# Attention with relative positions and a ternary layer: one PSUM bank moved from the small products to the logits, all places set anew

## The chip, the cores and the metric

The kernel runs on one core of a Trainium2 chip. The metric is the time of one launch on the device, in microseconds (us), as the median of several runs. The engines are TensorE (PE in the profile, with PEld for its weight loads, which overlap the products), VectorE (DVE), ScalarE (ACT), GpSimd (POOL) and SyncE (SP, whose queue issues the DMAs). Each works its own instructions strictly in order and waits on semaphores for the others. PSUM, the memory into which PE writes, has eight banks here, each of 128 partitions x 512 float32.

## The reference

Eight sequences of 1024 tokens with 256 features, 16 heads of 16, go through attention with learned relative positions (clipped at 64) and then through a linear layer with ternary weights; each has a layer norm ahead and behind.

```python
B, S, H, NH, MRP = 8, 1024, 256, 16, 64            # DK = 16
idx = clip(r[None, :] - r[:, None], -MRP, MRP) + MRP
rk, rv = embK[idx], embV[idx]                       # (S, S, DK)
q, k, v = heads(x @ Wq.T + bq), heads(x @ Wk.T + bk), heads(x @ Wv.T + bv)
logits = einsum('bhqd,bhkd->bhqk', q, k) + einsum('bhqd,qkd->bhqk', q, rk)
w = softmax(logits, axis=-1)
out = einsum('bhqk,bhkd->bhqd', w, v) + einsum('bhqk,qkd->bhqd', w, rv)
attn = out @ Wo.T + bo
x = x + layernorm(attn(layernorm(x)))
w_ternary = where(weight > delta, 1, where(weight < -delta, -1, 0))   # delta = 0.7 * mean(|weight|)
x = x + layernorm(layernorm(x) @ (w_ternary * alpha).T + bias)
```

## The kernel before

**Steps.** The attention runs over 128 steps: 8 sequences (batches) x 2 groups of 8 heads x 8 tiles of 128 queries. Four steps make a quad. A step s has these stages, and each is code in several engines' programs:

- row_max (s, p, half): PE multiplies keys and queries into the two banks of scores (L919); VectorE reduces each bank to a maximum per query, with the band of relative positions added (L1222, the near half) or without (L1216, the far half). There are eight such pairs of banks in a step.
- max_rows: PE turns the maxima (L929, into a misc bank), VectorE splits them into nm (L1235, L1237), and SyncE moves them into qs.
- weights (s, head, X or Y): PE makes a block of transposed logits for four or eight keys' tiles, four heads side by side, in a bank of logitsT (L946); the two nearest tiles get their band added through an identity product (L950). ScalarE takes the exponential into wl, wm, wr or wy (L1424) and so frees the bank. A half step has four X blocks, of which the first two are banded, and four Y blocks.
- weighted: PE multiplies the weights with the values into oacc (L970). merge: VectorE joins wl and wm (L1245).
- band_raw: PE makes the raw band terms for later steps in a misc bank (L902), ScalarE copies them twice into praw (L1403, L1404), and SyncE writes them to memory (bs, L785) and reads them back skewed (bands, L798).

Per quad come relative (L982, VectorE L1254), relative_sum (L995, VectorE adds it into oT, L1263) and out_norm (L1006, VectorE L1279). Beside the loop run the projections of the next batch in four chunks (turn_x L865, project_q and project_k L875, far L883, project_v L892 with VectorE's L1195) and the tail of each tile with both linear layers (tail_attT and tail_x1T L1020, tail_wo and tail_ff L1034 with VectorE's L1292 and L1333).

**PSUM.** The eight banks are NSCORE = 2 for scores, NLOG = 2 for logitsT, one for oacc and NMISC = 3 for misc. Scores and logits take their banks in turn. PE waits, before block n of logits, for exponential n - NLOG:

```python
lt = logitsT[block % NLOG]
pe.wait_ge(exp_ready, block + 1 - NLOG)
```

All small products (band_raw, max_rows, relative, relative_sum, out_norm, the projections, far and the four products of a tail; 993 uses of a bank in all) share the misc banks.

**The order.** Nothing is scheduled on the chip. The table PLACES gives every stage a place on a line, in slots of which a step has eight; timetable() lays all stages of all steps, chunks and tails out by it, and order_of() sorts them for each engine, with an offset for some stages on some engines (LAG, and END_LAG for the last four tiles). Each engine's program is its own sorted list. with_banks() goes through the same list and gives each small product the misc bank that comes free first. For that it assumes that a use holds its bank for HOLD[stage] slots; where no bank is free at its place, the stage and the rest of its chain are put off on the line:

```python
bank = until.index(min(until))
if until[bank] > slot:
    if chain:
        late[chain] = until[bank] - planned
    put_back((until[bank], i, planned, stage, k))
    continue
...
until[bank] = slot + (10 if stage == "relative" and k[2] < 3 else HOLD[stage])
```

HOLD and PLACES only set the order and the banks. On the chip PE always waits for the instruction that really frees the bank (misc_banks() makes that list from the plan, `pe.wait_ge(*free)`).

Of the kernel before, what the change touches and what calls it, by code (L numbers as in the profile page):

```python
# [11 lines left out]
ACT = mybir.ActivationFunctionType  # L12
# [33 lines left out]
LOWEST = -3.0e38  # L46
QRING, BRING, VRING, MRING = 5, 7, 3, 3
HB = HG // 2
NLOG, NMISC, NSCORE = 2, 3, 2


def tile_of(s):
# [51 lines left out]
def own_root(stage, k):  # L104
# [1 line left out]
    return k == (0, 0) if stage == "statistics" else last_tile(*k) and k[1] % 2 == 1  # L106


PLACES = {'chunk': (61.05, 71.03, 81.0, 91.0),
 'load_x': -8.23,  # L110
 'statistics': -5.34,
 'normalise': -2.6,
 'turn_x': 0.38,
 'project_q': 1.18,
 'project_v': 10.3,
 'far': 4.0,
 'write_q': 6.3,
 'project_k': 5.53,
 'write_far': 7.8,
# [4 lines left out]
 'first_stages': (-0.27, 0.5, 2.6, 4.4, 4.8, 5.83, 6.2, 6.3),  # L124
 'keys_first_stages': (0.0, 4.0, 4.8, 0.0, 3.0, 8.5, 7.3, 5.33),
 'first_load_k': (-84.0, -73.9, -63.8, -62.01),
 'first_load_q': (-89.0, -77.2, -65.4, -53.6),
 'first_raw': -54.47,
 'step': 7.2,
 'half': 3.55,  # L130
 'load_k': (-41.8, -33.8, -25.8, -17.8),
 'first_load_mk': (-83.9, -73.8, -63.8, -63.5),
 'load_mk': (-41.7, -33.7, -25.7, -17.7),
 'load_mq': -21.5,
 'first_load_mq': (-88.17, -77.1, -65.3, -53.5),
 'load_q': -32.7,
 'raw': (-28.8, -25.4),
 'band_write': (-26.3, -22.8),
 'band_read': (-22.18, -20.26),
 'row_max': (-12.49, -11.62, -10.75, -9.88, -9.01, -8.14, -7.1, -6.4),  # L140
 'max_reduce': -6.0,
 'max_rows': -4.88,
 'max_move': -5.05,
 'near': (0.0, 0.4, 0.72, 0.98),
 'rest': (1.76, 2.1, 2.5, 2.9),
 'value_x': 2.3,
 'value_y': 4.1,
 'merge': 3.2,
 'out_copy': 7.6,
 'relative': (29.57, 31.07),  # L150
 'piece_by': 0.35,
 'sum': (33.0, 33.95),
 'norm': (35.6, 36.59),
 'tail': 38.0,
 'tail_by': 8.0,
 'tail_late_by': 6.5,
 'tail_load': -1.0,
 'tail_attT': 0.21,
 'tail_wo': 1.0,
 'tail_x1': 3.0,  # L160
 'tail_norm': 3.5,
 'tail_normed': 5.4,
 'tail_x1T': 10.15,
 'tail_ff': 11.3,
 'tail_out': 13.5,
 'tail_store': 15.82,
 'end': 36.6,
 'end_by': 0.65,
 'end_stages': (0.3, 0.41, 2.27, 2.4, 3.4, 4.3, 4.7, 7.0, 6.8)}


def timetable():

    slots, x_ = [], PLACES

# [92 lines left out]
def with_banks(slots):  # L268
# [12 lines left out]
    while queue:  # L281
        slot, i, planned, stage, k = queue.pop()
        chain, bank = chain_of(stage, k), None
        if slot < planned + late.get(chain, 0):
            put_back((planned + late[chain], i, planned, stage, k))
            continue
        if stage in HOLD:
            if stage == "relative" and k[2]:
# [17 lines left out]
 'DVE': {'project_v': 0.17,  # L306
         'out_norm': 0.7,
         'tail_wo': 0.7,
         'tail_x1': 1.06,
         'tail_norm': 1.4,  # L310
         'tail_normed': 3.2,
         'tail_out': 1.9},
 'ACT': {'turn_x': -0.23, 'far': 0.4, 'project_q': 1.2, 'band_raw': -0.04},
 'POOL': {'project_q': 3.4,
          'project_k': 2.0,
          'far': 2.0,
# [6 lines left out]

END_LAG = {'PE': {},
 'SP': {},
 'DVE': {'tail_wo': 0.28, 'tail_ff': 0.5},
 'ACT': {'tail_attT': 0.2, 'tail_x1T': 1.0},
 'POOL': {'tail_wo': 0.95, 'tail_norm': 0.35, 'tail_ff': 0.86}}

# [1 line left out]
def order_of(engine, slots):  # L331


    def lag(stage, k):
# [25 lines left out]
HOLD = {'turn_x': 0.8,  # L360
 'project_q': 2.0,
 'project_k': 2.0,
 'far': 1.4,
 'project_v': 1.8,
 'band_raw': 0.8,
 'max_rows': 0.9,
 'relative': 1.0,
 'relative_sum': 1.4,
 'out_norm': 1.83,
 'tail_attT': 0.6,  # L370
 'tail_x1T': 0.5,
 'tail_wo': 1.3,
 'tail_ff': 1.3,
 'ternary': 2.0}


def counts(orders):
# [1186 lines left out]
```

## Time and profile before

| | |
|---|---|
| median of 3 runs | 2714.83 us (2706.01 to 2718.36) |
| the profiled execution | 2715.1 us |
| its span | 2713.3 us |
| TensorE busy | 2488.4 us, 92% |
| VectorE busy | 2098.3 us, 77% |
| ScalarE busy | 1563.9 us, 58% |
| GpSimd busy | 949.4 us, 35% |
| DMA engines busy with the main queue | 57.3% |

Busy times are of the whole span. The first 100 us are the start (constants, the first batch's projections, the first scores), the last 70 us the end of the last tiles; between them PE runs nearly full. A row of the timeline gives start and duration, the engine, the source line, the operation, output <- inputs by name and the count of merged instructions; in brackets stands the idle time before it and who ended that. Products are pipelined: neighbouring rows of PE overlap by up to some 0.1 us.

### The profile page before, as it was taken

To read this page: it belongs to the slowest core of one execution; us is meant where nothing else is said; L and a number is where in the kernel's file an instruction comes from. 1 tells how busy PE (TensorE), PEld (TensorE's weight loads), DVE (VectorE), ACT (ScalarE), POOL (GpSimd) and SP (SyncE) were. 2 spreads that over 40 slices of the span, in tenths; PEclk is the share of its full clock that TensorE was granted. 3 is DMA by queue.
4 is the path that set the end of the run, shared out by engine and by line. 5 is a ranking of instruction groups with operands and counts; after the bars stand their busy time and mean duration, and the time that the engine had idled before them with its cause. 6 is when DMAs were issued, how large, how long until landed. Compare 5 with 4: busy or idle time off the path is not lost. (4 is left out here: it accounts for less than half of the span.)

```text
span 2713.3 us, 101117 instructions
## 1 busy us (share of the span) xinstructions
PE 2488.4 (92%) x41858; PEld 1778.2 (66%) x41858; DVE 2098.3 (77%) x5306; ACT 1563.9 (58%) x2993; POOL 949.4 (35%) x2211
## 2 busy tenths in 40 slices
PE   5599999999999999999999999999999999999995
PEld 3266766667666676667666676666766667666664
DVE  5577778877888778877788777887778877787776
ACT  2266665566666555666556665556665655566652
POOL 3001533335342443424334253343524244341014
PEclk8699999999999999999999999999999999999997
DMA  6765674657656575566655666456764657656510
GB/s 162 210 162 160 184 185 132 163 161 204 167 148 168 156 196 155 148 164 178 183 140 157 172 187 177 138 145 167 209 168 132 164 168 192 164 141 178 142 42 29
DMA packets 696147, 434.22 MB, mean 160 GB/s; under 512 B 215847, under 2 KB 695431, under 8 KB 695559
## 3 DMA queue, kind: packets, MB, share of 16 engines
q1 hardware_dynamic: 695686, 427.75, 57.3%
q8 instruction: 330, 5.41, 0.9%
q14 instruction: 131, 1.07, 0.1%
HBM read 231.91 MB, written 194.92 MB: 157 GB/s over the span
## 5 line engine op out<-in xcount | busy, mean ns | idle before, releaser
L946 PE MATMUL logitsT<-qs,ks 98*128 98x128 bf16 (+1 forms) x8192 | 952.9, 222 | 31.5 <-ACT wr L1424 11.6
L1222 DVE CUSTOM_DVE_ANT_1 junk<-scores,bands 128x512 bf16<-128x512 f32 x988 | 680.3, 689 | 270.4 <-PE scores L919 115.4
L1424 ACT ACTIVATE wy<-logitsT 128x512 f32<-128x512 f32 x1024 | 589.5, 597 | 419.8 <-PE logitsT L946 408.7
L1216 DVE TENSOR_REDUCE maxes<-scores 128x1 f32<-128x512 f32 x1024 | 657.3, 683 | 173.3 <-PE scores L919 171.0
L946 PEld LDWEIGHTS logitsT<-qs,ks 98*128 98x128 bf16 (+1 forms) x8192 | 576.0, 99 | 306.6 <-issue 172.2
L919 PE MATMUL scores<-mks,mqs 48*128 48x256 bf16 (+6 forms) x3712 | 518.8, 291 | 121.1 <-DVE maxes L1216 62.5
L950 PE MATMUL logitsT<-ident,bands 128*128 128x128 f32 x2048 | 407.9, 280 | 0.0
L1424 ACT ACTIVATE wr<-logitsT 128x512 f32<-128x512 f32 x512 | 293.5, 596 | 163.6 <-PE logitsT L946 157.4
L919 PEld LDWEIGHTS scores<-mks,mqs 48*128 48x128 bf16 (+1 forms) x3712 | 162.9, 94 | 333.7 <-DVE maxes L1216 111.2
L1453 POOL TENSOR_SCALAR rs<-rs 128x1 int32<-128x1 int32 (+1 forms) x217 | 42.2, 195 | 898.9 <-DVE rs L1097 888.4
L950 PEld LDWEIGHTS logitsT<-ident,bands 128*128 128x128 f32 x2048 | 295.8, 144 | 24.9
L1458 POOL TENSOR_SCALAR rs<-rs 128x1 f32<-128x1 f32 x744 | 282.4, 382 | 64.9
L970 PE MATMUL oacc<-wy,vs 128*17 128x128 f32 (+1 forms) x9216 | 277.1, 264 | 0.7 <-ACT wy L1424 0.7
L1463 POOL TENSOR_SCALAR rs<-rs 128x1 f32<-128x1 f32 x744 | 217.5, 295 | 66.1
L970 PEld LDWEIGHTS oacc<-wy,vs 128*17 128x17 f32 x9216 | 207.1, 98 | 37.5 <-issue 9.4
L1424 ACT ACTIVATE wl<-logitsT 128x512 f32<-128x512 f32 x256 | 158.4, 619 | 117.7 <-PE logitsT L950 116.4
L1424 ACT ACTIVATE wm<-logitsT 128x512 f32<-128x512 f32 x256 | 154.3, 603 | 83.0 <-PE logitsT L950 78.4
L1403 ACT ACTIVATE praw<-misc 128x512 f32<-128x512 f32 x256 | 153.4, 599 | 64.7 <-DMA bs<-praw 44.0
L1245 DVE COPY_PREDICATED wm<-later,wl 128x512 f32<-128x512 int32 x224 | 175.7, 784 | 2.2 <-PE oacc L970 2.2
L970 PE MATMUL oacc<-wr,vs 128*17 128x128 f32 (+1 forms) x4608 | 161.6, 264 | 0.0
L1404 ACT ACTIVATE praw<-misc 128x512 f32<-128x512 f32 x256 | 156.3, 611 | 0.0
L970 PEld LDWEIGHTS oacc<-wr,vs 128*17 128x17 f32 x4608 | 118.1, 100 | 0.1
(147 smaller groups left out, 2977.5 us busy)
## 6 DMA issues: line engine op xcount, KB each, us to landing
bs<-praw SPq DMA_DIRECT2D x256, 512.0 KB, 4.3
bands<-bs SPq DMA_DIRECT2D x224, 512.0 KB, 4.4
ks<-kd SPq DMA_DIRECT2D x64, 384.0 KB, 4.8
qs<-qd SPq DMA_DIRECT2D x112, 192.0 KB
bands<-bs SPq DMA_DIRECT2D x128, 128.0 KB, 3.3
mks<-kd SPq DMA_DIRECT2D x128, 96.0 KB, 3.9
qd<-qparts SPq DMA_DIRECT2D x60, 192.0 KB, 2.6
kd<-kparts SPq DMA_DIRECT2D x60, 192.0 KB, 2.6
```

The source lines that it names most:

```text
L919: mm = e.matmul(scores[(u + side) % NSCORE][:, c % 512:c % 512 + length], mqs[i][HALF * side:HALF * side + depth, p, :], kk[HALF * side:HA ...
L946: mm = e.matmul(lt[:, j * P:(j + 1) * P], kk[0:depth, SLOT[HB * blk + j], kt * P:(kt + 1) * P], qs[i][0:depth, SLOT[HB * blk + j], :], sta ...
L950: mm = e.matmul(lt[:, j * P:(j + 1) * P], band[v % BRING][:, j, c * P:(c + 1) * P], ident[:], start=False, stop=True, is_transpose=True, s ...
L970: mm = e.matmul(oacc[32 * j:32 * j + VW, o0 + q0:o0 + q1], vs[m_ % VRING][:, int(right), kt, h, :], src, start=first and c == 0, stop=True ...
L1216: e.tensor_reduce(top, sc[:], AX.X, ALU.max).then_inc(row_maxed, 1)
L1222: e.tensor_tensor_reduce(junk[:], sc[:].rearrange("p (a c) -> p a c", a=2), banded, 1.0, LOWEST, ALU.add, ALU.max, top).then_inc(row_maxed, 1)
L1245: e.copy_predicated(right, mask.bitcast(I32), left).then_inc(merged, 1)
L1403: e.activation(dst[:, :, 0:P], src, ACT.Copy)
L1404: e.activation(dst[:, :, P:WIN], src[:, :, P - 1:P].broadcast_to([P, HB, P]), ACT.Copy).then_inc(praw_ready, 1)
L1424: e.activation(dst, src, ACT.Exp).then_inc(exp_ready, 1)
L1458: op = e.tensor_scalar(rs[k][:, 3, x:x + 1], rs[k][:, 2, x:x + 1], rs[k][:, 0, x:x + 1], rs[k][:, 2, x:x + 1], ALU.mult, ALU.mult)
L1463: op = e.tensor_scalar(rs[k][:, 2, x:x + 1], rs[k][:, 3, x:x + 1], 1.5, rs[k][:, 2, x:x + 1], ALU.add, ALU.mult)
```

## The change

Three things are changed, all in tables of numbers. The code of the engines is the same.

- NLOG becomes 3 and NMISC 2. The sum stays at eight banks.
- HOLD is shortened for every stage (band_raw from 0.8 to 0.2 slots, project_q from 2.0 to 1.25, out_norm from 1.83 to 0.75, relative_sum and tail_ff to slightly negative values), so with_banks() accepts a new use of a bank soon after the last one.
- PLACES, LAG and END_LAG get new numbers. Most move by under 0.5 slots. The second block of an X series moves behind the third ('near'), far, the chunks' places and the first loads of mks and mqs move as well.

```diff
-NLOG, NMISC, NSCORE = 2, 3, 2
+NLOG, NMISC, NSCORE = 3, 2, 2
...
- 'near': (0.0, 0.4, 0.72, 0.98),
- 'rest': (1.76, 2.1, 2.5, 2.9),
+ 'near': (0.0, 0.76, 0.72, 0.98),
+ 'rest': (1.76, 2.1, 2.5, 2.77),
...
-HOLD = {'turn_x': 0.8,
- 'project_q': 2.0,
+HOLD = {'turn_x': 0.06,
+ 'project_q': 1.25,
...
- 'relative_sum': 1.4,
- 'out_norm': 1.83,
+ 'relative_sum': -0.12,
+ 'out_norm': 0.75,
```

What this makes of the order shows at three places on PE. The first is the first series of logits, step 0. The numbers behind the names are those of the banks. Before:

```order
L919 MATMUL scores1<-mks0,mqs1 128x256
L946 MATMUL logitsT1<-qs0,ks0 128x128
L950 MATMUL logitsT1<-ident,bands 128x128
...
L946 MATMUL logitsT0<-qs0,ks0 128x128 x4
L919 MATMUL scores0<-mks0,mqs1 128x384
...
L946 MATMUL logitsT1<-qs0,ks0 128x128 x4
L946 MATMUL logitsT0<-qs0,ks0 128x128 x4
```

After:

```order
L919 MATMUL scores1<-mks0,mqs1 128x256
L946 MATMUL logitsT1<-qs0,ks0 128x128 x4
L946 MATMUL logitsT2<-qs0,ks0 128x128
L950 MATMUL logitsT2<-ident,bands 128x128
...
L919 MATMUL scores0<-mks0,mqs1 128x384
...
L946 MATMUL logitsT0<-qs0,ks0 128x128 x4
L946 MATMUL logitsT1<-qs0,ks0 128x128 x4
```

The banded block (L946 and L950 in turn) and the plain block have changed places, and the blocks go round three banks.

The second place is the end of a quad while the next batch is projected (step 72; max_rows is that of step 73). L995 is relative_sum, L929 max_rows. Before:

```order
L919 MATMUL scores1<-mks1,mqs2 128x256
L995 MATMUL misc1<-relout,relsel 32x4x32 x16
L946 MATMUL logitsT1<-qs2,ks1 128x128 x4
L970 MATMUL oacc<-wl0,vs0 17x128 x4
L970 MATMUL oacc<-wm,vs0 17x128 x4
L970 MATMUL oacc<-wr,vs0 17x128 x8
L929 MATMUL misc2<-ident,negmax1 8x128
L946 MATMUL logitsT0<-qs2,ks1 128x128 x4
L875 MATMUL misc0<-xnT,wk 128x256 x4
```

After:

```order
L946 MATMUL logitsT2<-qs2,ks1 128x128 x4
L883 MATMUL misc0<-qf,farw 32x128 x4
L995 MATMUL misc1<-relout,relsel 32x4x32 x16
L970 MATMUL oacc<-wl0,vs0 17x128 x4
L970 MATMUL oacc<-wm,vs0 17x128 x4
L970 MATMUL oacc<-wr,vs0 17x128 x8
L929 MATMUL misc1<-ident,negmax1 8x128
L946 MATMUL logitsT0<-qs2,ks1 128x128 x4
L946 MATMUL logitsT1<-qs2,ks1 128x128 x4
```

far (L883) has come between the two relative_sums, and max_rows now takes the bank that relative_sum has just filled; before it took another one.

The third place is the start. The order of the products is the same, the banks are not. These are the band_raw products (L902) of steps 1 to 3, before:

```order
L902 MATMUL misc1<-bandtab,qs1 128x128 x4
L902 MATMUL misc0<-bandtab,qs1 128x128 x4
L902 MATMUL misc2<-bandtab,qs2 128x128 x4
...
L902 MATMUL misc1<-bandtab,qs2 128x128 x4
...
L902 MATMUL misc0<-bandtab,qs3 128x128 x4
```

After:

```order
L902 MATMUL misc0<-bandtab,qs1 128x128 x4
L902 MATMUL misc1<-bandtab,qs1 128x128 x4
L902 MATMUL misc0<-bandtab,qs2 128x128 x4
...
L902 MATMUL misc1<-bandtab,qs2 128x128 x4
...
L902 MATMUL misc0<-bandtab,qs3 128x128 x4
```

The last one, band_raw (3, 0), follows in its bank on band_raw (1, 1) before and on band_raw (2, 0) now.

## Rows read from the trace of the kernel before

**Rows 1.** The page's first part: busy us (share of the span) x instructions.

```profile
PE 2488.4 (92%) x41858; PEld 1778.2 (66%) x41858; DVE 2098.3 (77%) x5306; ACT 1563.9 (58%) x2993; POOL 949.4 (35%) x2211
```

**Rows 2.** Stretch, us; PE, PEld, DVE, ACT, POOL busy; granted clock, DMA share, GB/s.

```profile
420.00:740.00 320.00, 304.70 (x5220) 219.40 (x5217) 255.63 (x644) 194.17 (x372) 125.17 (x286) 0.99 0.61 168
```

**Rows 3.** Waits of PE: line waited for: us in total, times, longest.

```profile
PE scores L919 <- DVE maxes L1216: 62.5, 200, 1.6
PE scores L919 <- DVE maxes L1222: 28.4, 65, 2.9
...
PE logitsT L946 <- ACT wr L1424: 11.6, 41, 0.5
...
PE logitsT L946 <- ACT wy L1424: 3.4, 12, 0.6
...
PE logitsT L946 <- ACT wm L1424: 2.2, 4, 0.6
...
PE oacc L970 <- ACT wy L1424: 0.7, 1, 0.7
```

**Rows 4.** Waits of PE's weight loads at the logits.

```profile
PEld logitsT L946 <- ACT wr L1424: 72.9, 237, 0.7
```

**Rows 5.** Waits of VectorE for scores.

```profile
DVE maxes L1216 <- PE scores L919: 171.0, 253, 3.0
```

**Rows 6.** Timeline of PE, two Y blocks of step 75.

```profile
1614.14 0.39 PE L946 MATMUL logitsT<-qs,ks 101*128 101x128 bf16 x4
1614.46 0.39 PE L919 MATMUL scores<-mks,mqs 48*128 48x256 bf16 x4
1614.78 0.40 PE L946 MATMUL logitsT<-qs,ks 101*128 101x128 bf16 x4
1615.72 0.40 PE L946 MATMUL logitsT<-qs,ks 98*128 98x128 bf16 x4 [0.54 <-ACT wr L1424]
```

**Rows 7.** Timeline of ScalarE, the same stretch.

```profile
1614.34 0.84 ACT L1381 ACTIVATE qf<-misc,bk 128x256 f32<-128x256 f32 x2 [1.19 <-PE misc L875]
1615.07 0.60 ACT L1424 ACTIVATE wr<-logitsT 128x512 f32<-128x512 f32 x1
```

**Rows 8.** Timeline of PE, relative_sum and max_rows at step 72.

```profile
1556.53 1.08 PE L995 MATMUL misc<-relout,relsel 128*32 128x128 f32 x32
...
1558.87 0.27 PE L929 MATMUL misc<-ident,negmax 128*8 128x128 f32 x1
```

**Rows 9.** Timeline of VectorE, the same stretch.

```profile
1559.34 0.69 DVE L1263 TENSOR_TENSOR oT<-misc,oT 128x512 f32<-128x512 f32 x1
```

**Rows 10.** Timeline of PE, project_v and the next tail_wo.

```profile
1651.31 1.89 PE L892 MATMUL misc<-wv,xnT 128*128 128x256 f32 x8
...
1656.37 1.13 PE L1034 MATMUL misc<-wo,rowsT 128*128 128x256 f32 x4
```

**Rows 11.** Timeline of VectorE there.

```profile
1655.24 1.41 DVE L1195 TENSOR_TENSOR vs<-misc,bvs 128x256 f32<-128x256 f32 x4
```

**Rows 12.** Timeline of PE near the end of the start.

```profile
90.63 0.61 PE L902 MATMUL misc<-bandtab,qs 96*128 96x128 bf16 x4
```

**Rows 13.** Timeline of ScalarE there.

```profile
98.97 0.59 ACT L1404 ACTIVATE praw<-misc 128x512 f32<-128x512 f32 x1
```

**Rows 14.** Timeline of VectorE there.

```profile
94.88 0.17 DVE L1229 TENSOR_REDUCE negmax<-maxes 128x8 f32<-128x16 f32 x1
102.19 0.69 DVE L1222 CUSTOM_DVE_ANT_1 junk<-scores,bands 128x512 bf16<-128x512 f32 x1 [7.14 <-DMA bands<-bs]
...
103.65 0.27 DVE L1235 CAST nm<-misc 8x128 bf16<-8x128 f32 x1
```

**Rows 15.** As rows 2, a stretch after several waits for scores.

```profile
1209.50:1213.00 3.50, 3.50 (x35) 2.50 (x27) 2.15 (x6) 2.06 (x4) 2.99 (x10) 0.50 0.00 0
```

**Rows 16.** Timeline of PE, eight products before and in it.

```profile
1203.91 0.62 PE L946 MATMUL logitsT<-qs,ks 101*128 101x128 bf16 x8
...
1209.65 1.03 PE L946 MATMUL logitsT<-qs,ks 101*128 101x128 bf16 x8
```

More of the change, by code:

```diff
@@ L106, in own_root @@
     return k == (0, 0) if stage == "statistics" else last_tile(*k) and k[1] % 2 == 1
-PLACES = {'chunk': (61.05, 71.03, 81.0, 91.0),
+PLACES = {'chunk': (61.72, 71.69, 81.66, 91.62),
  'load_x': -8.23,
@@ L112 @@
  'normalise': -2.6,
- 'turn_x': 0.38,
+ 'turn_x': 0.25,
  'project_q': 1.18,
- 'project_v': 10.3,
- 'far': 4.0,
+ 'project_v': 10.09,
+ 'far': 4.52,
  'write_q': 6.3,
@@ L123 @@
  'first_normalise': (-103.3, -99.5, -89.5, -79.5),
[L124 to L127, printed above, removed]
+ 'first_stages': (-0.3, 0.47, 2.57, 4.15, 4.77, 5.8, 6.17, 6.83),
+ 'keys_first_stages': (0.0, 4.0, 4.8, 0.08, 3.0, 8.5, 7.3, 5.33),
+ 'first_load_k': (-83.61, -73.9, -63.8, -62.01),
+ 'first_load_q': (-89.0, -77.2, -64.9, -53.6),
  'first_raw': -54.47,
@@ L130 @@
  'half': 3.55,
- 'load_k': (-41.8, -33.8, -25.8, -17.8),
- 'first_load_mk': (-83.9, -73.8, -63.8, -63.5),
- 'load_mk': (-41.7, -33.7, -25.7, -17.7),
+ 'load_k': (-41.8, -33.8, -25.8, -17.84),
+ 'first_load_mk': (-83.13, -73.03, -63.03, -62.73),
+ 'load_mk': (-41.8, -33.7, -25.7, -17.91),
  'load_mq': -21.5,
- 'first_load_mq': (-88.17, -77.1, -65.3, -53.5),
+ 'first_load_mq': (-83.18, -73.73, -61.06, -50.13),
  'load_q': -32.7,
  'raw': (-28.8, -25.4),
- 'band_write': (-26.3, -22.8),
+ 'band_write': (-26.51, -22.8),
  'band_read': (-22.18, -20.26),
@@ L143 @@
  'max_move': -5.05,
- 'near': (0.0, 0.4, 0.72, 0.98),
- 'rest': (1.76, 2.1, 2.5, 2.9),
+ 'near': (0.0, 0.76, 0.72, 0.98),
+ 'rest': (1.76, 2.1, 2.5, 2.77),
  'value_x': 2.3,
- 'value_y': 4.1,
+ 'value_y': 4.12,
  'merge': 3.2,
- 'out_copy': 7.6,
+ 'out_copy': 7.74,
  'relative': (29.57, 31.07),
- 'piece_by': 0.35,
- 'sum': (33.0, 33.95),
- 'norm': (35.6, 36.59),
+ 'piece_by': 0.37,
+ 'sum': (33.44, 34.25),
+ 'norm': (35.47, 36.59),
  'tail': 38.0,
@@ L157 @@
  'tail_load': -1.0,
- 'tail_attT': 0.21,
+ 'tail_attT': -0.28,
  'tail_wo': 1.0,
@@ L161 @@
  'tail_norm': 3.5,
- 'tail_normed': 5.4,
+ 'tail_normed': 5.5,
  'tail_x1T': 10.15,
@@ L167 @@
  'end': 36.6,
- 'end_by': 0.65,
- 'end_stages': (0.3, 0.41, 2.27, 2.4, 3.4, 4.3, 4.7, 7.0, 6.8)}
+ 'end_by': 0.66,
+ 'end_stages': (0.3, 0.41, 2.11, 2.32, 3.4, 4.16, 4.7, 7.0, 6.85)}
 def timetable():
@@ L308 @@
          'tail_wo': 0.7,
-         'tail_x1': 1.06,
+         'tail_x1': 0.88,
          'tail_norm': 1.4,
@@ L312 @@
          'tail_out': 1.9},
- 'ACT': {'turn_x': -0.23, 'far': 0.4, 'project_q': 1.2, 'band_raw': -0.04},
+ 'ACT': {'turn_x': -0.23, 'far': 0.4, 'project_q': 1.2, 'band_raw': -0.13},
  'POOL': {'project_q': 3.4,
@@ L325 @@
  'SP': {},
- 'DVE': {'tail_wo': 0.28, 'tail_ff': 0.5},
+ 'DVE': {'tail_wo': 0.28, 'tail_ff': 0.5, 'tail_norm': 0.22, 'tail_x1': -0.12},
  'ACT': {'tail_attT': 0.2, 'tail_x1T': 1.0},
@@ L359 @@
             "tail_wo": "lin_ready", "tail_ff": "lin_ready", "ternary": "threshold_ready"}
-HOLD = {'turn_x': 0.8,
- 'project_q': 2.0,
[L362 to L367, printed above, removed]
- 'relative_sum': 1.4,
- 'out_norm': 1.83,
[L370 to L374, printed above, removed]
+HOLD = {'turn_x': 0.06,
+ 'project_q': 1.25,
+ 'project_k': 0.92,
+ 'far': 0.45,
+ 'project_v': 0.45,
+ 'band_raw': 0.2,
+ 'max_rows': 0.23,
+ 'relative': 0.25,
+ 'relative_sum': -0.12,
+ 'out_norm': 0.75,
+ 'tail_attT': 0.15,
+ 'tail_x1T': 0.12,
+ 'tail_wo': 0.75,
+ 'tail_ff': -0.34,
+ 'ternary': 0.5}
 def counts(orders):
```

## Prediction

> **What bounds the kernel now.** The page's busy times come first: TensorE (PE) is busy for 2488.4 of 2713.3 us, VectorE for 77% and ScalarE for 58% of the span [rows 1]. The table by stretches says how this is spread: in 320 us from the middle, PE is busy for 304.70 us and VectorE for 255.63 us [rows 2]. So over most of the span the kernel is bound by PE's in-order queue, and only that about 5% in which PE stands still can be won by better buffering. The waits of PE say what ends those gaps. The largest are for VectorE, which must have read a bank of scores before PE may write it again: 62.5 and 28.4 us. Those for ScalarE to have read a bank of logits are 11.6, 3.4 and 2.2 us, together 17.2 us in 57 places [rows 3]. The same waits seen by PE's weight loads (PEld), which run ahead of the products, are longer: 72.9 us in 237 places for wr alone [rows 4], where the products show 11.6 us in 41. VectorE in turn waits for PE's scores, 171.0 us at the far half alone [rows 5]: neither is always behind.
>
> The change moves one PSUM bank from misc to logitsT and leaves scores at two. It adds and removes no matmul, activation, reduction or transfer. So the time can change in three ways alone: waits for a logits bank go, waits for a misc bank come, and the moved steps meet other neighbours. I sum these against the profiled execution's own 2715.1 us; the median of the runs shown, 2714.83 us, is 0.3 us below it, so nothing has to be converted.
>
> **Term 1, the third logits bank.** A block of four products that is not held up starts 0.32 us before the next work: 1614.14 to 1614.46. At 1614.78 such a block starts, and the next one follows only at 1615.72, 0.94 us later, with 0.54 us shown as idle and ended by ScalarE's wr [rows 6]. So a gap costs what is shown plus about 0.08 us, the overlap of two groups that is lost with it. ScalarE was late there because two copies of project_k's result, from 1614.34 on, stood ahead of the exponential that frees the bank; that one ran from 1615.07 for 0.60 us [rows 7]. With three banks the block at 1615.72 needs the bank of the exponential before that one, which was done before those copies began. I compared, for all blocks between 100 and 2640 us, the start of the weight load with the end of the exponential two and three blocks back: with two banks about 400 of some 2,000 reach PE with their bank not yet free or free for less than 0.15 us; with the third one none does, and the smallest margin is over 0.4 us. So the term is 17.2 us + 57 x 0.08 us = 21.8 us, and I take **-22 us**. It could be as small as the 17.2 us shown, and as large as 22 us plus 0.08 us for each of the 237 - 41 = 196 places where only the weight load waited for wr, 38 us. I take the lower value since in those places the trace shows no idle time of the products. ScalarE's queue is not made longer by this, it is fed earlier.
>
> **Term 2, two misc banks in the steady part.** A small product now takes the bank of the second small product before it, not of the third. With three banks the trace has next to none of these waits outside the start. What two would do is read from when each bank was freed. The clearest place: relative_sum of the second block (32 products) starts at 1556.53, and max_rows starts at 1558.87 [rows 8]; VectorE adds the sum into oT only from 1559.34 for 0.69 us, since it has two score reductions ahead of it [rows 9]. In the changed order these two have the same bank, misc1, while before max_rows took misc2, which was long free. So max_rows would wait from 1558.87 to 1560.03, 1.16 us. Queued behind it on PE are two blocks of logits and the next scores. This pattern returns once in each of the seven batches whose projections run beside the loop: 7 x 1.16 = 8.1 us. The second place is tail_wo of a batch's first tile: it starts at 1656.37 [rows 10], and project_v's bank is freed at 1655.24 + 1.41 = 1656.65 [rows 11]: 0.28 us, or 2.0 us in all, if the two keep their times. But project_v held its bank from 1651.31 on [rows 10], 5.34 us, and the changed order puts only 4.1 us of PE work between the two; if the bank is held as long, it is 1.2 us each time, 8.6 us in all. In the same way, by each bank's time from its product to its release and the work that the changed order puts between, max_rows to band_raw is 7 x 0.76 = 5.3 us, max_rows to out_norm is 14 x 0.33 = 4.7, turn_x to band_raw 7 x 0.47 = 3.3, and band_raw to turn_x 7 x 0.26 = 1.8 us. In these it is a question whether the bank is freed earlier once the step is moved. The ends are therefore 0 (if later places in VectorE's and ScalarE's queues free the banks in time) and 8.1 + 8.6 + 5.3 + 4.7 + 3.3 + 1.8 = 32 us. I take **+8 us**, the one pattern that shows in full both by the old times and by the new distances; the others are near to nothing by the old times.
>
> **Term 3, the start.** Before the loop PE issues the band_raw products of four steps ahead, and ScalarE can copy them only as the writes to bs land. band_raw (3, 0) was at 90.63, in a bank that had been free for long. In the changed plan it takes the bank of band_raw (2, 0), which ScalarE leaves at 98.97 + 0.59 = 99.56 [rows 12, 13]. PE then stands for 9 us, and behind it are the last scores of step 0. From 90.63 to the end of that step's negmax VectorE and PE needed 95.05 - 90.63 = 4.4 us, and the next two score reductions another 1.5 us (102.19 to 103.65); then VectorE makes nm, at 99.56 + 4.4 + 1.5 = 105.5 instead of 103.65 [rows 14]. Most of the 9 us is hidden, since VectorE waited 7.14 us for bands until 102.19 anyway. I take **+2 us**, with the ends 0 and 9. The reordered loads of mqs and mks on SyncE's queue carry the same transfers between the same neighbours ahead of the first scores; I cost that at nothing, within 1 us.
>
> **Edits costed at nothing.** The banded blocks of a series are now issued as 0, 2, 1, 3 instead of 0, 1, 2, 3. It is the same work, and it brings weighted Y nearer to the exponential it needs; there PE waited for ScalarE once, 0.7 us [rows 3], and a band_raw, a banded block and one score step, some 1.4 us of PE work, still lie between. If that cover were gone, 128 places at 0.1 us would be 13 us. SyncE and the queue of GpSimd (one addition past one root at the end) move by steps within their own idle time. END_LAG concerns the last four tiles alone, which I cost at nothing within 2 us either way.
>
> The sum is 2715.1 - 22 + 8 + 2 = 2703.1 us.
>
> **Rivals.** (a) More of the logits waits count, down to term 1's far end: 2715.1 - 38 + 8 + 2 = 2687 us; with term 2 at nothing too, 2679 us. For it speak the 72.9 us of PEld, against it that PE's products show 17.2 us. (b) The wait only changes its name: PE comes earlier to the next scores, whose two banks are the same, and waits there for VectorE instead. The trace has 265 such waits [rows 3], for some 1,000 score steps, so about one gap in four would swallow what is won before it; if all did, 2715.1 + 8 + 2 = 2725 us. Against it speak the 171 us in which VectorE waits for PE: an earlier PE also makes VectorE earlier. A page of the Trainium skill, TensorE: Matmul & The Clock Gate (section HAM oscillation — how this bites in real kernels), reports a kernel to which PSUM double-buffering brought no further gain; by that rule it would be this 2725 us, and no run here shows it yet. (c) **Slower**: the misc waits come in full. Two banks for 993 small products mean one new product per bank each 5.1 us, and a relative_sum holds its own for 3.5 us, from 1556.53 to 1560.03 [rows 8, 9]. If VectorE and ScalarE free them no earlier than now, term 2 is 32 us and term 3 up to 9: 2715.1 - 22 + 32 + 9 = 2734 us. It decides against the change from a total of 22 us, 0.022 us per small product. The granted clock can add to it. After a stretch of waits for scores it was 0.50, the lower level of 1.2 GHz, for 3.5 us [rows 15]; there eight products of logits took 1.03 us instead of 0.62 us [rows 16], so such a stretch costs 3.5 x (1 - 0.62 / 1.03) = 1.4 us, and one more in each batch some 10 us. The same page (section A second HAM failure mode: psum-queue depth-cycling) says that short idle times between groups of products, as PE cycles through its banks, make the clock swing. Whether two misc banks bring such swings no row here can show.
>
> **How the numbers follow.** The summed case has a chance of 0.60 and lies within 2690 to 2718 us; about 0.35 of it is below 2701.3 us and 0.25 above. Rival (a) has 0.10, (b) 0.10, (c) 0.20. What a measurement of this kernel can tell from no change is about 0.5%, 13.6 us: 2701.3 to 2728.4. Faster than that is 0.35 + 0.10 = 0.45, within it 0.25 + 0.10 = 0.35, slower 0.20. The prediction is the time of the summed case, 2703 us. The range leaves out the outer part of (a) and of (c), a tenth on each side: 2680 to 2738 us.
>
> **What would show it.** In the profile of the changed kernel PE's and PEld's waits at logitsT for ScalarE should all but vanish (the one of PEld for wr under 5 us, from 72.9). At the misc lines new waits should stand: max_rows (L929) for oT, seven times about 1.1 us, one of some 9 us for praw at band_raw (L902) near 90 us, and little else, 20 us in all. PE's waits for maxes should stay at 80 to 100 us. If they grow by 15 us or more, (b) holds; if the misc lines together show over 30 us, (c). PE's busy time should stay at 2488 us within 10; if it moves by more, the clock did it. The prediction is wrong in its ground if the logits waits stay, or if the time moves by more than these lines of waits account for.

## The result, and the profile after

The changed kernel took 2669.84 us in the median of four runs (2661.24 to 2674.08), the kernel before 2710.73 us (2706.01 to 2718.36) beside it: a ratio of 0.9842, 95% interval 0.9804 to 0.9881. It is 41 us faster. I had predicted 2703 us, and 2669.84 lies below the range of 2680 to 2738. A second comparison of the same pair gave 0.9847 [0.9821, 0.9873]. One execution is left out of the table below, a slow one: of e12's ten it took 4207.69 us, against 2690 to 2708 us for the other nine.

The profiled execution took 2672.93 us, of which the span is 2670.7. First the page's busy times, the answer to [rows 1]:

```profile
PE 2457.5 (92%) x41858; PEld 1783.3 (67%) x41858; DVE 2081.4 (78%) x5306; ACT 1557.1 (58%) x2993; POOL 946.8 (35%) x2211
```

PE's share is the same 92%, but its busy time fell by 31 us with the same 41858 instructions. I had said that this number would stay within 10. Then the waits of PE, the answer to [rows 3], with the largest ones at the small products:

```profile
PE scores L919 <- DVE maxes L1216: 68.6, 221, 1.1
PE scores L919 <- DVE maxes L1222: 40.5, 96, 0.8
PE misc L902 <- ACT praw L1404: 13.1, 3, 9.5
...
PE misc L875 <- DVE vs L1195: 7.8, 2, 5.2
PE oacc L970 <- ACT wr L1424: 4.1, 17, 0.2
```

No wait of the products for a logits bank is left. The waits for scores rose from 90.9 to 109.1 us. No wait of max_rows (L929) for oT is in the list. The weight loads at the logits, the answer to [rows 4]:

```profile
PEld logitsT L946 <- ACT wy L1424: 15.0, 69, 0.4
PEld logitsT L946 <- ACT wm L1424: 4.5, 21, 0.2
PEld logitsT L946 <- ACT wr L1424: 3.9, 18, 0.2
```

The 72.9 us for wr are 3.9. Not all of these waits vanished, as I had said they would: those for wy fell only from 20.3 to 15.0 us, and the three together from 106.5 to 23.4. Last, one row of the page's costliest groups. Its columns are busy us, mean ns of one, and the idle time just before the group. First the kernel before, then the changed one:

```profile
L946 PE MATMUL logitsT<-qs,ks 98*128 98x128 bf16 (+1 forms) x8192 | 952.9, 222 | 31.5 <-ACT wr L1424 11.6
```

```profile
L946 PE MATMUL logitsT<-qs,ks 98*128 98x128 bf16 (+1 forms) x8192 | 887.5, 221 | 0.0
```

The same 8192 products are busy for 65.4 us less, and the mean of one is nearly the same: the busy time of a group counts stretches in which any of its products is in flight, and they lie closer now. 31.5 us of idle time ahead of them are gone as well. That is 97 us at this line, and the kernel gained 41. Such a sum overstates the gain, since blocks that now follow each other directly overlap in it: e1 below already has 914.8 and 20.5 us here, 49 less than before, and its time is only 12 us shorter. So the experiments compare whole times, and starts at a fixed order.

The start came out as announced. PE stands 9.53 us at band_raw (3, 0):

```profile
99.90 0.59 PE L902 MATMUL misc<-bandtab,qs 96*128 96x128 bf16 x4 [9.53 <-ACT praw L1404]
...
104.58 0.37 PE L929 MATMUL misc<-ident,negmax 128*8 128x128 f32 x1
```

VectorE makes the first nm at 105.94 us (before 103.65 [rows 14], I had said 105.5), and the first logits start at 115.5 instead of 112.7 us.

### The profile page after: what moved, and what is told of

Its sections match the earlier page's. It is cut to its first block, busy times and chain, and to the rows that moved or that the text cites. A ratio compares the mean times of both kernels' runs of the same rounds, so it can differ in the third digit from the quotient of the medians.

```text
span 2670.7 us, 101092 instructions
## 1 busy us (share of the span) xinstructions
PE 2457.5 (92%) x41858; PEld 1783.3 (67%) x41858; DVE 2081.4 (78%) x5306; ACT 1557.1 (58%) x2993; POOL 946.8 (35%) x2211
## 4 chain that ended last, share of the span: by engine, by line
PE 30%; DVE 16%; issue 4%; POOL 2%; ACT 1%; DMA 0%; SPq 0%; DVEq 0%; POOLq 0%; ACTq 0%
PE oacc L970 7%; PE logitsT L946 6%; PE scores L919 6%; DVE maxes L1216 5%; DVE junk L1222 4%; PE logitsT L950 3%; PE misc L875 2%; PE misc L1034 2%; DVE stats L1092 1%; PE misc L982 1%; PE misc L892 1%; PE misc L995 1%; PE misc L902 1%; DVE mv L1095 1%; POOL rs L1458 1%
## 5 line engine op out<-in xcount | busy, mean ns | idle before, releaser
L946 PE MATMUL logitsT<-qs,ks 98*128 98x128 bf16 (+1 forms) x8192 | 887.5, 221 | 0.0
L1424 ACT ACTIVATE wy<-logitsT 128x512 f32<-128x512 f32 x1024 | 579.9, 599 | 371.3 <-PE logitsT L946 360.7
L946 PEld LDWEIGHTS logitsT<-qs,ks 98*128 98x128 bf16 (+1 forms) x8192 | 574.8, 99 | 201.4 <-issue 150.3
L919 PE MATMUL scores<-mks,mqs 48*128 48x256 bf16 (+6 forms) x3712 | 523.0, 292 | 124.1 <-DVE maxes L1216 68.6
L1424 ACT ACTIVATE wr<-logitsT 128x512 f32<-128x512 f32 x512 | 305.5, 597 | 237.7 <-PE logitsT L946 230.7
L950 PE MATMUL logitsT<-ident,bands 128*128 128x128 f32 x2048 | 412.2, 279 | 0.0
L1453 POOL TENSOR_SCALAR rs<-rs 128x1 int32<-128x1 int32 (+1 forms) x217 | 50.6, 233 | 880.1 <-DVE rs L1097 870.6
L950 PEld LDWEIGHTS logitsT<-ident,bands 128*128 128x128 f32 x2048 | 294.4, 144 | 21.0
L1245 DVE COPY_PREDICATED wm<-later,wl 128x512 f32<-128x512 int32 x224 | 168.3, 751 | 1.5 <-PE oacc L970 1.5
L902 PE MATMUL misc<-bandtab,qs 96*128 96x128 bf16 x1024 | 101.0, 221 | 17.3 <-ACT praw L1404 13.1
```

The source lines that it names most:

```text
L919: mm = e.matmul(scores[(u + side) % NSCORE][:, c % 512:c % 512 + length], mqs[i][HALF * side:HALF * side + depth, p, :], kk[HALF * side:HA ...
L946: mm = e.matmul(lt[:, j * P:(j + 1) * P], kk[0:depth, SLOT[HB * blk + j], kt * P:(kt + 1) * P], qs[i][0:depth, SLOT[HB * blk + j], :], sta ...
L950: mm = e.matmul(lt[:, j * P:(j + 1) * P], band[v % BRING][:, j, c * P:(c + 1) * P], ident[:], start=False, stop=True, is_transpose=True, s ...
L1245: e.copy_predicated(right, mask.bitcast(I32), left).then_inc(merged, 1)
L1424: e.activation(dst, src, ACT.Exp).then_inc(exp_ready, 1)
```

## The experiments

Two things had to be told apart: what the banks did, and what the new places did. The places again have two parts, since one entry of the table alone (`near`) gives the order of the four blocks of a series, and with it their neighbours. Where a kernel has another number of misc banks than its order was planned with (e2, e3, e12 and e15 with two, e4 and e13 with three), each small product takes the bank that has been unused the longest; a plan made anew would have moved the products too. All results together, each beside runs of the kernel before on the same chip:

| kernel | places | series | logits / misc / scores banks | ratio | 95% |
|---|---|---|---|---|---|
| changed | new | 0,2,1,3 | 3 / 2 / 2 | 0.9842, 0.9847 | 0.9804 to 0.9881, 0.9821 to 0.9873 |
| e1 | new | 0,2,1,3 | 2 / 2 / 2 | 0.9956 | 0.9940 to 0.9972 |
| e4 | new | 0,2,1,3 | 2 / 3 / 2 | 0.9948 | 0.9930 to 0.9966 |
| e13 | new | 0,1,2,3 | 2 / 3 / 2 | 0.9998 | 0.9982 to 1.0014 |
| e7 | new | 0,1,2,3 | 3 / 2 / 2 | 0.9929 | 0.9909 to 0.9949 |
| e3 | old | 0,1,2,3 | 2 / 2 / 2 | 1.0087 | 1.0063 to 1.0111 |
| e2 | old | 0,1,2,3 | 3 / 2 / 2 | 0.9987 | 0.9970 to 1.0004 |
| e8 | old | 0,2,1,3 | 2 / 3 / 2 | 0.9976 | 0.9961 to 0.9992 |
| e12 | old | 0,2,1,3 | 3 / 2 / 2 | 0.9947 | 0.9927 to 0.9966 |
| e17 | new | 0,2,1,3 with the neighbours of before | 3 / 2 / 2 | 0.9890 | 0.9866 to 0.9914 |
| e16 | new | 0,1,2,3 with the new neighbours | 3 / 2 / 2 | 0.9865 | 0.9838 to 0.9892 |
| e11 | new, one step moved | 0,2,1,3 | 3 / 2 / 2 | 0.9826 | 0.9796 to 0.9857 |
| e9 | new | 0,2,1,3 | 2 / 2 / 3 | 0.9465 | 0.9443 to 0.9486 |
| e15 | old | 0,1,2,3 | 2 / 2 / 3 | 0.9651 | 0.9619 to 0.9683 |

### The banks, at the order of work of each kernel

e1, the changed kernel without the third logits bank:

```diff
-NLOG, NMISC, NSCORE = 3, 2, 2
+NLOG, NMISC, NSCORE = 2, 2, 2
```

> The changed kernel, every instruction in its changed order and on its two misc banks, with two logits banks instead of three (one PSUM bank stays empty). It measures the third logits bank alone, at a fixed order. Theory A (the bank is worth more than the 22 us of my first term, since waits of the weight loads also stood in the blocks that I took as not held up): about 2710 us, the whole gain gone, and PEld's waits at logitsT for ScalarE back at 70 us or more. Theory B (the bank is worth the 22 us, and the rest of the gain of 41 us is the new order's): 2688 to 2694 us.

e4, the changed order with the banks of before:

```diff
-NLOG, NMISC, NSCORE = 3, 2, 2
+NLOG, NMISC, NSCORE = 2, 2, 2
+BANKS = 3
...
+            bank = min((i for i in range(BANKS) if i != held), key=lambda i: used[i])
```

> The changed order with the banks of before: two for logits, three for misc. Beside the first run of this set it measures the third misc bank in the new order, and beside the kernel before the new places alone. If the new places are what frees the misc banks in time, it is within 5 us of the first run. Theory A: 2705 to 2712 us, the places alone are worth nothing. Theory B: about 2690 us.

e3 and e2, the order of before with one misc bank less, and with that bank given to the logits:

(NMISC stays what the order is planned with, BANKS is what is really given out.)

```diff
 NLOG, NMISC, NSCORE = 2, 3, 2
+BANKS = 2
...
+            bank = min((i for i in range(BANKS) if i != held), key=lambda i: used[i])
```

```diff
-NLOG, NMISC, NSCORE = 2, 3, 2
+NLOG, NMISC, NSCORE = 3, 3, 2
+BANKS = 2
...
```

> The kernel before in its old order with two logits banks and two misc banks (one PSUM bank stays empty). It measures what the missing third misc bank costs where nothing was moved. My second and third term: 2710 + 10 = 2720 us as summed, 2751 us at the far end. Theory A says nothing of it. If VectorE and ScalarE free the banks in time anyway: 2710 to 2715 us, with only the wait of 9 us at the start in PE's waits.

> The kernel before, every engine in its old order, with three logits banks and two misc banks; the misc banks are given out to the one that was used longest ago. It measures the moved bank without any new place. Theory A: 2675 to 2690 us, most of the gain, less 8 to 20 us of waits at the misc lines. Theory B: 2700 to 2710 us. By my second term in full (32 us of misc waits) it would be 2720 us.

Medians against their own runs of before: e1 -12.0 us, e4 -15.3, e3 +22.2, e2 -3.2. The 2698 us of e1 lie between my two theories: the bank is worth more than 22 us and less than the whole gain. e4 is nearer to theory B, e2 in its range, and the 2732 us of e3 lie between the sum and the far end that I had named. So a third logits bank is worth 25 us in the old order (e3 to e2) and 28 to 29 in the new one (e1 to changed). The missing misc bank costs 22 us in the old order and 3 in the new one, where the intervals of e1 and e4 overlap, so that it can't be told from nothing. These are e3's new waits (its lines past 440 are ten higher: L912 is band_raw's line, L885 that of project_q and project_k):

```profile
PE misc L912 <- DVE vs L1205: 11.1, 14, 1.2
...
PE misc L885 <- DVE oT L1273: 5.0, 7, 0.7
```

They stand in 14 and 7 places, twice and once in each of the seven batches whose projections run beside the loop. In the changed kernel L902 doesn't wait for VectorE at all, and L875 does so in two places of the start.

e1 and the changed kernel issue exactly the same products in the same order, so each interval from one start to the next can be compared, from step 4 to step 116. Summed by the work that starts at its end: logits -49.6 us, weighted sums +12.3, scores +9.6, the rest +4.6; together -23.1 us (2239.5 to 2216.4). From e3 to e2 it is logits -47.5, scores +12.3, weighted +10.1, together -24.4. The bank gave about 50 us at the logits, and half was given back one or two groups later, at scores (VectorE has not yet read the bank) and at the weighted sums (ScalarE has not yet written the weights). The page's own rows show the first half of this. Here is L946 of e1, to be held against 887.5 and 0.0 above:

```profile
L946 PE MATMUL logitsT<-qs,ks 98*128 98x128 bf16 (+1 forms) x8192 | 914.8, 221 | 20.5 <-ACT wr L1424 9.1
```

27.3 us of busy and 20.5 of idle time are gone with the bank, 47.8 us. And the waits of e1 for scores, against the 68.6 and 40.5 us of the changed kernel, show some of the second half:

```profile
PE scores L919 <- DVE maxes L1216: 60.9, 195, 1.0
PE scores L919 <- DVE maxes L1222: 35.8, 82, 0.8
```

The other part stands in the weight loads of the weighted sums. This row is in the changed kernel and has no counterpart in e1:

```profile
PEld oacc L970 <- ACT wr L1424: 15.7, 56, 0.4
```

### The order within a series

e8 and e7: one line of the table, put into the kernel before, and taken out of the changed one.

```diff
- 'near': (0.0, 0.4, 0.72, 0.98),
+ 'near': (0.0, 0.76, 0.72, 0.98),
```

```diff
- 'near': (0.0, 0.76, 0.72, 0.98),
+ 'near': (0.0, 0.4, 0.72, 0.98),
```

> The kernel before with one number changed: the second block of an X series goes behind the third (near: 0.76 for 0.4). Banks as before. Theory C (the new series order, banded and plain blocks in turn, makes the 15 us that the new places gave at the old banks): 2693 to 2699 us. Theory D (the gain is that of the other places, which let VectorE and ScalarE free banks and feed PE sooner): 2706 to 2712 us, no measurable change.

> The changed kernel with that one number set back: blocks 0, 1, 2, 3 in order. Three logits banks, two misc banks. Theory C: 2682 to 2688 us, 12 to 18 us slower than the changed kernel. Theory D: within 4 us of the changed kernel's 2670 us.

e8 came out as theory D had it (2708.63 us) and e7 as neither: 2696.38 us, a larger loss than C's. e12 and e13 complete the set of all combinations of the three parts: the series and the moved bank without the other places, and the other places alone. (The lines that give out BANKS are those of e3.)

```diff
- 'near': (0.0, 0.4, 0.72, 0.98),
+ 'near': (0.0, 0.76, 0.72, 0.98),
-NLOG, NMISC, NSCORE = 2, 3, 2
+NLOG, NMISC, NSCORE = 3, 3, 2
+BANKS = 2
...
```

```diff
- 'near': (0.0, 0.76, 0.72, 0.98),
+ 'near': (0.0, 0.4, 0.72, 0.98),
-NLOG, NMISC, NSCORE = 3, 2, 2
+NLOG, NMISC, NSCORE = 2, 2, 2
+BANKS = 3
...
```

> The kernel before with the moved bank and the new series order, all other places old. Three parts are now told apart: the moved bank (alone 0.9987 of before), the series order (alone 0.9976), the other places. Theory E (the series order pays with three banks, about 23 us as measured in the changed kernel, and 7 us with two): 0.990, 2684 to 2692 us. Theory F (the parts add up, 3 + 7 us): 0.996, 2700 to 2705 us.

> The other places alone: new places, lags and holds, but the old series order, and the banks of before. New places and series order together gave 0.9948 at these banks, the series order alone 0.9976. If they add up, 0.997 to 0.998. If the other places only pay by freeing the two misc banks in time, 0.999 to 1.001.

> The changed kernel once more, beside the kernel before and the next three, to have its ratio on the same chip as theirs. Expected 0.984 to 0.986.

Alone, the moved bank gives 0.13%, the series 0.24%, the other places 0.02%: 0.4% in sum. Together they give 1.5%. The interval of e12, 0.9927 to 0.9966, holds theory F's 0.996 and not E's 0.990; e13 shows no gain of the other places by themselves. The series is worth 7 us in the old places (e8), 13 in the new ones with the old banks (e13 to e4), and 22 with three logits banks (e7 to changed). The other places are worth nothing alone, and 25 us once series and bank are there (2699.64 us, the median of e12's nine, to 2674.62 us of the changed kernel beside it). Most of that is the misc bank, whose loss costs 22 us at the old places and 3 at the new ones.

Why is the series worth anything? The entry moves block 1 from 0.4 to 0.76, and two things change: the order of the blocks, and what stands between them. Two theories: **H**, the order, by which a long banded block and a short plain one come in turn; **G**, the neighbours. In the trace of the changed kernel a plain block of four logits products is followed after 0.23 us where the next group uses the whole array too, and after 0.32 us where it divides the array by rows (scores, 48 or 51 partitions for each half) or by columns (weighted sums):

```profile
1558.06 0.39 PE L946 MATMUL logitsT<-qs,ks 101*128 101x128 bf16 x4
1558.29 0.61 PE L865 MATMUL misc<-ident,xc 128*128 128x128 f32 x4
...
1559.52 0.39 PE L919 MATMUL scores<-mks,mqs 51*128 51x256 bf16 x4
1559.85 0.40 PE L946 MATMUL logitsT<-qs,ks 101*128 101x128 bf16 x4
1560.08 1.95 PE L875 MATMUL misc<-xnT,wq 128*128 128x256 f32 x8
1561.86 0.39 PE L946 MATMUL logitsT<-qs,ks 101*128 101x128 bf16 x4
1562.18 0.39 PE L919 MATMUL scores<-mks,mqs 48*128 48x256 bf16 x4
```

The first column is the start: 1558.06 to 1558.29 and 1559.85 to 1560.08 are 0.23 us, 1561.86 to 1562.18 is 0.32. Over all such pairs from step 4 to step 116 the medians are 0.226 us (plain block to plain block, 287 pairs) and 0.224 (to band_raw, 140), against 0.322 (to scores, 336) and 0.332 (to weighted sums, 152); after a banded block 0.695 (to a plain block) against 0.790 and 0.792. So after a block of logits a change of the array's division costs about 0.095 us. A scores group of two 512-column products is followed after 0.32 us by a group divided by columns (35 pairs) and by one on the whole array (87 pairs) alike, so a change from rows straight to columns is counted as one. The Trainium skill has this as a rule, without a price: TensorEngine Tiling (Array Packing), section Key Properties, says that a change of the tiling mode drains TensorE. The trace agrees in so far as a change costs these 0.095 us; whether it is a drain no row shows. Counted in the traces over the three kinds of groups (whole array, by rows, by columns), the kernel before makes 3065 changes, the changed kernel 2942 and the changed kernel with the old series 3069. The counts in the two expectations below differ a little from these; the 127 between them are the same. So G says 127 x 0.095 = 12 us for the series in the new places. e17 has the new order of blocks with the old neighbours (3116 changes), e16 the old order with the new neighbours (2989):

```diff
- 'near': (0.0, 0.76, 0.72, 0.98),
+ 'near': (0.0, 0.76, 0.4, 0.98),
```

```diff
- 'near': (0.0, 0.76, 0.72, 0.98),
+ 'near': (0.0, 0.72, 0.76, 0.98),
```

> The changed kernel with the blocks in the new order 0, 2, 1, 3, but with the old neighbours: block 2 before weighted and block 1 behind it, so PE changes 3116 times, as in the kernel without the new series order. Theory G: 0.989 to 0.994, the 127 changes more cost 12 us at least. Theory H: 0.984 to 0.987, no loss.

> The changed kernel with the blocks of an X series in the old order 0, 1, 2, 3, but with the new neighbours: weighted comes before block 1, and blocks 1 and 2 stand together. PE changes between kinds of groups 2989 times, as in the changed kernel. Theory G (the number of changes between full-array groups and tiled groups counts, about 0.1 us each): within 6 us of the changed kernel, 0.984 to 0.987 of before. Theory H (the order of banded and plain blocks counts): 0.991 to 0.994, like the changed kernel without the new series order.

With old neighbours the two orders have 0.9929 (e7) and 0.9890 (e17), with new ones 0.9865 (e16) and 0.9847. Read down, the neighbours are worth 0.64% and 0.43%, 17 and 12 us; read across, the order is worth 0.39% and 0.18%, 11 and 5 us. Both runs lie in the ranges of theory G, e17 at the edge of it. H alone is refuted: e16 has the old order and keeps three quarters of the gain. The order's share is near to what these intervals can tell, and why it exists is open.

G alone doesn't hold either. Putting the new series into the kernel before (e8) takes out the same 127 changes, 3065 to 2938, and so does each other pair that differs by the series alone. G says 12 us for each. The four pairs gave 7 us (before to e8), 11 (e2 to e12), 13 (e13 to e4) and 22 (e7 to changed). So what a change costs between two groups doesn't pass into the kernel's time as it is: the rest of the order and the banks decide how much of it is kept. Which wait takes or gives the difference these runs don't show.

Part of these small differences is the clock. The mean granted clock was 0.971 in the executions of e7 and e17, 0.976 in those of e16, 0.975 in those of e8 and 0.971 in those of before beside e8. Among executions of one and the same kernel the time falls by about 1.9 us for each 0.001 of mean granted clock (a line through all that the table rests on, with a level of its own for each kernel and chip). Taken to an equal clock by that, an estimate, the neighbours are worth 9 to 10 us in both orders and the order 11 to 12 us with both neighbours, each within some 4 us, and e8 gains nothing (it is 1 us slower, within 2). The four pairs then spread from a loss of 1 us to a gain of 21, so the clock doesn't explain why they differ. It may itself follow from the order.

### The start

e11 puts the one held band_raw behind max_rows:

```diff
-                at(w0 + x if s else x_["first_raw"] + 12.5 + x, stage, s, blk)
+                at(-4.8 if (stage, s, blk) == ("band_raw", 3, 0) else w0 + x if s else x_["first_raw"] + 12.5 + x, stage, s, blk)
```

> The changed kernel with one product moved: band_raw of step 3, first block, which waited 9.5 us at the start for its misc bank, stands behind max_rows of step 0. By the working of my third term the first logits come 2 us earlier, 2668 us; if the wait was hidden, 2670 us. The 9.5 us must be gone from PE's waits either way.

The wait of 9.5 us is gone and another has come in front of max_rows:

```profile
PE misc L929 <- ACT praw L1404: 5.1, 1, 5.1
```

The first logits start at 113.8 instead of 115.5 us, and the span is 2670.7 in both. The comparison, 0.9826 against 0.9842 and 0.9847, can't tell 2 us from nothing, so neither of the two cases that I had named is shown.

### The bank where PE waits longest

In [rows 3] the largest waits by far were for scores, and the change did not lessen them (90.9 us before, 109.1 after). e9 and e15 give the bank taken from misc to the scores instead, in the new order and in the old one:

```diff
-NLOG, NMISC, NSCORE = 3, 2, 2
+NLOG, NMISC, NSCORE = 2, 2, 3
```

```diff
-NLOG, NMISC, NSCORE = 2, 3, 2
+NLOG, NMISC, NSCORE = 2, 3, 3
+BANKS = 2
```

> The changed order with the freed bank given to the scores: two logits banks, three scores banks, two misc banks. It tells whether PE's largest waits, those for VectorE at the scores (109 us in the changed kernel), are a matter of buffers. If they are: below the 2698 us of two and two banks by more than the 28 us that the third logits bank gave, 2640 to 2670 us. If VectorE itself is behind in these places and a third bank only moves the wait by one score: 2685 to 2698 us.

> The old order with two logits, three scores and two misc banks. In the changed order the third scores bank brought the time from 0.9956 to 0.9465 of before. If that is a matter of the buffer and not of places, the old order goes from 1.0087 (two, two and two banks) by about 0.045 to 0.955 to 0.970. If it needs the new places: above 0.985.

e9 takes 2569.69 us, 146 us less than before and 134 less than e1, from which it differs by this bank alone; e15 takes 116 us less than e3. e15 lies in the range that I expected for a matter of the buffer; e9 gained far more than the 2640 to 2670 us that I had named for it. e9 is the fastest kernel found here. Its waits and busy times:

```profile
PE scores L919 <- DVE maxes L1216: 12.7, 39, 0.9
PE scores L919 <- DVE maxes L1222: 10.7, 22, 1.0
...
PE logitsT L946 <- ACT wr L1424: 9.8, 39, 0.9
PE logitsT L946 <- ACT wy L1424: 6.2, 19, 0.6
```

```profile
PE 2410.5 (94%) x41858; PEld 1746.7 (68%) x41858; DVE 2072.6 (81%) x5306; ACT 1564.1 (61%) x2993; POOL 953.3 (37%) x2211
```

The waits for scores fell from 96.7 us in e1 to 23.4, by 73, and PE's busy time from 2478.8 to 2410.5, by 68. The products' waits named the right bank and gave a little over half of its worth. The weight loads' waits come nearer here, if not at the logits, where they fell by 77 us (100.1 in e1, 23.4 in the changed kernel) for 50. Here are those of e1 and then of e9 at the scores, 196.5 and 59.4 us, 137 less:

```profile
PEld scores L919 <- DVE maxes L1216: 107.1, 268, 1.2
PEld scores L919 <- DVE maxes L1222: 89.4, 217, 1.3
```

```profile
PEld scores L919 <- DVE maxes L1222: 30.0, 66, 1.3
PEld scores L919 <- DVE maxes L1216: 29.4, 80, 1.0
```

The products' waits for ScalarE at the logits hardly grew (14.8 us in e1, 16.2 in e9), and those at the weighted sums rose from 0.9 to 5.0 us: little took the place of the scores waits. That fits VectorE (81%) and ScalarE (61%) having room, which wasn't tested by itself. The clock helped a little: the stretches at 1.2 GHz sum to 126 us in e1's profile and 107 in e9's, by [rows 15, 16] about 8 us of the 134, an estimate. A kernel with three banks for both would need a ninth bank, or one misc bank; that wasn't tried.

## Why the prediction was wrong, step by step

**What bounds the kernel.** Right as far as it went: PE's queue, with VectorE's reads of the scores as the largest wait. The sentence that "only that about 5% in which PE stands still can be won by better buffering" is wrong. e9 won 5.4% by buffering with 23 us of scores waits still there, and half of it came out of PE's busy time.

**Term 1, -22 us.** The mechanism is right and the size too small: 25 and 28 us net where I had 22. The working was wrong by more than that, in two parts that cancel. What the bank gives at the logits is 48 to 50 us, above even my far end of 38, which was rival (a)'s; net of what was given back it stays below that. I had dropped the places where only the weight load waits, as "in those places the trace shows no idle time of the products". But a late weight load also sets the next products apart without a shown gap: a plain block behind a plain block starts 0.329 us later on average in e1 and 0.229 in the changed kernel, over 287 pairs, and a plain block behind a banded one 0.853 and 0.695, over 77. Also the 0.32 us that I took from [rows 6] for "a block that is not held up" was a block ahead of scores, and has the change of the array's division in it; ahead of another block it is 0.23.

**Rival (b), the wait changes its name.** I gave it 0.10 as an all-or-nothing case, and priced it as one gap in four. It was true for nearly half: of 50 us, 22 were given back at scores and weighted sums. The waits for scores rose by 18 us, over the 15 I had set, and yet the bank paid.

**Term 2, +8 us.** Too large here. The place it rested on, relative_sum and the next max_rows in bank misc1, is this in the changed kernel, on PE and on VectorE:

```profile
1540.49 1.06 PE L995 MATMUL misc<-relout,relsel 128*32 128x128 f32 x32
...
1542.45 0.27 PE L929 MATMUL misc<-ident,negmax 128*8 128x128 f32 x1
```

```profile
1540.95 0.69 DVE L1222 CUSTOM_DVE_ANT_1 junk<-scores,bands 128x512 bf16<-128x512 f32 x1
...
1541.61 0.69 DVE L1263 TENSOR_TENSOR oT<-misc,oT 128x512 f32<-128x512 f32 x1
...
1543.28 0.40 DVE L1092 BATCH_NORM_STATS2 stats<-xc 128x6 f32<-128x256 f32 x1
```

VectorE adds into oT 1.12 us after the product's start, not 2.81 us as in [rows 8, 9]; the bank is free at 1542.30, and max_rows starts at 1542.45. After the product's start one whole score reduction stands ahead of the addition and not two. And the statistics of the next chunk's layer norm, which now come behind it, stood ahead of both reductions before. My working had passed over them:

```profile
1556.47 0.74 DVE L1092 BATCH_NORM_STATS2 stats<-xc 128x6 f32<-128x256 f32 x2
1557.25 0.40 DVE L1095 BATCH_NORM_AGGREGATE mv<-stats 128x2 f32<-128x6 f32 x2
1557.68 0.30 DVE L1097 TENSOR_SCALAR rs<-mv 128x2 f32<-128x2 f32 x1
1557.90 0.68 DVE L1222 CUSTOM_DVE_ANT_1 junk<-scores,bands 128x512 bf16<-128x512 f32 x1
```

They took from 1556.47 to 1557.98, 1.5 us of the 2.81. I had taken the time at which VectorE frees the bank from the old order, while the change moved VectorE's queue too (`sum` from 33.0 to 33.44, `chunk` by 0.62 to 0.67). With the old order terms 2 and 3 together would have been 22 us (e3), in the middle of the 0 to 41 us that I had named for them. In the new one they measured 3 us (e4 to e1), where I had 10. All waits of the products at misc lines rose by 10 us, from 61.8 to 71.4, and the one wait of the third term is 9.5 of that.

**Term 3, +2 us.** The mechanism is right: a 9.53 us wait as announced, nm at 105.94 instead of 105.5. That the whole kernel loses 2 us by it is not shown (e11).

**Edits costed at nothing.** This is the step that failed by most. "It is the same work" is true of the sum of the products' times, and not of PE's time: what stands next to what costs about 0.095 us per change of the array's division, and the order of banded and plain blocks has a share of its own, whose mechanism is open. The series brought 13 us with the old banks and 22 with three logits banks. I listed what it would cost if a cover were gone (13 us) and no gain at all: the range had no term below nothing for it.

**The sum.** 2715.1 - 22 + 8 + 2 = 2703.1. By the runs: the other places 0 to -2, the series -13, the lost misc bank +3, the logits bank -28, together -40 us (unrounded), 2675, against 2672.93 of the profiled execution.

**Rival (c)** is refuted for this order; in the old one, where e3 shows +22 us, its misc waits are real. Its addition, the clock, played no part between the two kernels: the stretches in which the granted clock is at 1.2 GHz sum to 157 us in the profile of before and 162 in that of the changed kernel. The sentence "if it moves by more, the clock did it" on PE's busy time was wrong; the products lie closer. The finding on double-buffering in the Trainium skill's TensorE: Matmul & The Clock Gate, section HAM oscillation — how this bites in real kernels, which is of one other kernel, did not carry over: by it a third bank would have given nothing, and here it gave 25 to 28 us, and 134 for scores. The swings of the clock that the same page's section A second HAM failure mode: psum-queue depth-cycling tells of did not grow with two misc banks: between 150 and 2640 us the stretches at 1.2 GHz sum to 54 us before and 44 after. The Trainium skill's Perfetto Trace Analysis, section Identifying Performance Opportunities, has the rule that fits: the same gap repeating on the engine that should be busy can mean too few buffers. The scores waits, 200 and 65 times in [rows 3], were that gap.

## What to carry to other kernels

Give a spare bank to the wait that is largest in the list of the bounding engine. In the two cases here the gain lay between the fall of the products' waits and that of the weight loads' waits (scores: 73 and 137 us, gain 134; logits: 20 and 77 us, gain 28 after nearly half was given back). Then ask which wait comes next. When a table of places changes, cost the neighbours: count how often TensorE's queue changes between groups that divide the array differently, and read when each bank is freed from the changed queue of the engine that frees it, not from the old one. Parts that are worth nothing alone (the other places, 0.02%) can be what makes another part pay, so measure such a change whole, or in all combinations of its parts. And before a difference of a few us is given a cause, compare the granted clocks of the runs.

## What was not expected of the hardware

A change between a group of products on the whole array and one that divides it by rows or columns costs about 0.095 us: 0.226 and 0.224 us from start to start without it, 0.322 and 0.332 with it, over 915 pairs. If all of the some 3000 changes in this kernel cost that, it is about a tenth of its time; but where 127 of them were taken out, 7 to 22 us came of it and not the same 12 each time.

PE's busy time is not a constant of the work. With the same 41858 instructions it was 2488.4 us before, 2457.5 changed, and 2410.5 in e9, with the mean of one logits product at 222, 221 and 221 ns. Before and changed have the same granted clock (0.971 and 0.970); e9 had 0.980, which by [rows 15, 16] is worth some 20 us of its 78 (157 us at 1.2 GHz before, 107 in e9), an estimate. The falls went with shorter waits of the weight loads for a bank: at the logits from 106.5 us (72.9, 20.3 and 13.3) to 23.4 in the changed kernel, at the scores from 183.4 us before to 59.4 in e9. That is not all of it: e7 has 24.8 us of these waits at the logits and is busy for 2475.1 us, so the series has a part in the changed kernel's 2457.5.
